# Two loads of residual rows and one set of weight casts take another place in a gated block's first feed-forward pass

## The reference, cut to what matters

```python
h = xn @ Wff1                              # 512 -> 2 x 2048
a, gate = h[..., :ff_inner], h[..., ff_inner:]
out = out + silu(gate) * a @ Wff2          # 2048 -> 512
x = x + tanh(g_xattn) * out
```

## Time and profile before

| | us |
|---|---|
| median of three executions | 2398.21 |
| the profiled execution, device time | 2401.12 |
| its span | 2399.3 |
| PE busy | 2127.6 |
| DVE busy | 1335.9 |
| ACT busy | 673.2 |
| POOL busy | 622.9 |

### The profile page before, as it was taken

How to read it: one execution, slowest core, us unless ns; L and a number is a source line. 1 busy time by engine, 2 the same in 40 slices (tenths; PEclk the granted TensorE clock), 3 DMA queues, 4 the chain that set the end, 5 groups by cost and what they waited for, 6 DMA issues and landing times. The chain is left out here.

```text
span 2399.3 us, 30019 instructions
## 1 busy us (share of the span) xinstructions
PE 2127.6 (89%) x11425; PEld 1593.7 (66%) x11425; DVE 1335.9 (56%) x2112; ACT 673.2 (28%) x1066; POOL 622.9 (26%) x552
## 2 busy tenths in 40 slices
PE   6999999999989999999999999998998435465898
PEld 5677777777668778888888888887873111121477
DVE  7665666566447777666766676666661000000377
ACT  2544554455533331112111211122430000000231
POOL 5434654464458850320032000000320000000020
PEclk9899999999999999999999999998998767687899
DMA  4223223311387659664966494434879999999767
GB/s 156 76 102 126 73 77 111 129 62 62 106 322 294 231 218 371 226 223 158 364 223 223 159 369 159 160 127 149 316 275 430 427 427 428 428 428 426 290 228 263
DMA packets 182380, 565.13 MB, mean 236 GB/s; under 512 B 15304, under 2 KB 98792, under 8 KB 152392
## 3 DMA queue, kind: packets, MB, share of 16 engines
q1 hardware_dynamic: 172936, 504.37, 55.7%
q10 hardware_dynamic: 9312, 58.99, 6.0%
HBM read 450.07 MB, written 113.25 MB: 235 GB/s over the span
## 5 line engine op out<-in xcount | busy, mean ns | idle before, releaser
L1444 PE MATMUL ff_down<-w,u 128*128 128x512 f32 x1536 | 363.7, 395 | 9.4 <-DVE ff_x L1717 9.3
L1384 PE MATMUL ff_up<-ff_t,w 128*128 128x512 f32 x1488 | 357.7, 389 | 2.3 <-ACT ff_gate L1517 2.3
L1444 PEld LDWEIGHTS ff_down<-w,u 128*128 128x128 f32 x1536 | 292.1, 191 | 74.7 <-DVE ff_x L1717 13.6
L1384 PEld LDWEIGHTS ff_up<-ff_t,w 128*128 128x128 f32 x1488 | 279.2, 188 | 60.6 <-issue 2.7
L1717 DVE SCALAR_TENSOR_TENSOR ff_x<-ff_down,gates,ff_x 128x512 f32<-128x512 f32 x256 | 191.1, 749 | 88.1 <-PE ff_down L1444 86.5
L2500 PE MATMUL e_down<-e_w,e_ug 128*32 128x512 f32 x480 | 76.7, 797 | 183.8 <-DMA e_w<-in_L_ffn_e_W 104.0
L1384 PE MATMUL ff_up<-ff_b,w 128*128 128x512 f32 x954 | 234.3, 389 | 0.0
L1384 PEld LDWEIGHTS ff_up<-ff_b,w 128*128 128x128 f32 x954 | 179.1, 188 | 37.2
L2500 PEld LDWEIGHTS e_down<-e_w,e_ug 128*32 128x32 f32 x480 | 18.7, 141 | 240.6 <-issue 131.1
L1509 ACT ACTIVATE ff_gate<-ff_gate 128x512 f32<-128x512 f32 x62 | 39.2, 633 | 410.9 <-DVE ff_gate L1693 410.9
L2604 DVE TENSOR_TENSOR e_u_rows<-e_turned,e_b1T 128x128 f32<-128x128 f32 x16 | 4.7, 292 | 266.4 <-PE e_turned L2491 266.4
(11 more groups left out here) (449 smaller groups left out, 4307.3 us busy)
## 6 DMA issues: line engine op xcount, KB each, us to landing
w<-ff_w_factors SPq DMA_DIRECT2D x48, 1792.0 KB, 7.6
e_wg<-in_L_ffn_e_Wg SPq DMA_DIRECT2D x15, 4096.0 KB, 29.1
e_w<-in_L_ffn_e_W SPq DMA_DIRECT2D x14, 4096.0 KB, 24.1
e_w<-in_L_ffn_e_W ACTq DMA_DIRECT2D x13, 4096.0 KB, 49.8
ff_w_factors<-w SPq DMA_DIRECT2D x15, 1792.0 KB, 7.2
w<-ff_w_parts SPq DMA_DIRECT2D x48, 512.0 KB, 5.3
ff_t<-ff_t_factors SPq DMA_DIRECT2D x16, 1024.0 KB, 13.9
e_w<-in_L_ffn_e_W SPq DMA_DIRECT2D x16, 1024.0 KB, 10.1
```

The costliest lines, as they stand in the source:

```text
L1384: last = nc.tensor.matmul(bank[:, :], a, m, start=start and c == 0, stop=stop and c == 5)
L1444: last = nc.tensor.matmul(DN[m % 2][:, :], a, w, start=c == 0, stop=c == 5)
```

## The change

Two things move in the first feed-forward pass. SP waits for the stores of x1 and issues both `load_x(0, i)` ahead of `keep_w1(0)`, where these came behind `keep_w1(2)`. ACT does `high_a(3)`, the casts of the fourth group's weights, behind `finish(2)`, that is behind the gates of groups 1 and 2, where they stood ahead of both; `high_s(3)`, which stood between `group(2, True)` and `finish(2)`, now follows it.

```diff
@@ sync
             for i in (S2_T2, S1_T1, S3_T3, A22_T4):
                 load_factor(i, 0)
+            x1_out, all_stores = x1_begun
+            sp.wait_ge(x1_out, all_stores)
+            for i in range(2):
+                load_x(0, i)
             keep_w1(0)
...
             load_raw(4)
             keep_w1(2)
-            x1_out, all_stores = x1_begun
-            sp.wait_ge(x1_out, all_stores)
-            for i in range(2):
-                load_x(0, i)
             keep_w2(0)
@@ scalar
             group(1, True)
+            group(2, True)
+            finish(2)
             high_a(3)
-            group(2, True)
             high_s(3)
-            finish(2)
             high_w2(2)
```

## The result

The changed kernel took 2409.01 us, median of 7 executions (2400.22 to 2412.20), against 2398.21 us (2394.54 to 2405.01) for the kernel before. The ratio is 1.0033, 95% interval 1.0022 to 1.0044. It is slower by some 8 us, where 2400.5 us was forecast.

The account below looks back on a forecast made before the run. PE, busy 89% of the span, was taken to bound the feed-forward stage. +0.3 us at group 3 and +2.0 at down(1) on 2401.12 gave 2403.4, less 2.9 for the median 2400.5 us; range 2393.5 to 2405.5.

Parts of the forecast that it names:

- The first wait, for ACT: At group 2's fourth product, PE's 2.27 us wait for ACT's silu goes, with 0.1 us of clock.
- The row loads and their price: At down(0), the 3.12 us wait for rows goes, but PE stops 6.0 us for POOL; group 3 starts 0.3 us later.
- The push on the raw weights: In the DMA queue, two early row loads make group 3's raw weights land 5.3 us later, at 704.55.
- the clock's cost: In down(0), the clock falls behind the 6.0 us stop and costs 1.7 us, bounds 0.1 and 3.4.
- What is late next: ACT's gates of group 3 come 2.6 us late, so PE waits 2.0 us in down(1), bounds 0 and 3.1.
- R3: Rival, chance 0.15: POOL falls behind, PE also waits for low parts of groups 3 and 4; 2404.6 us, 2406 with another clock fall.
- The range: For the whole kernel's time, 8 in 10: 2393.5 to 2405.5 us, allowing 2 us for differing medians.
- The sign behind 1668 us: A stage behind 1668 us changing its length by more than 1 us would make the whole sum wrong.
- R1: Rival, chance 0.27: the late gates don't reach PE, no wait in down(1); +0.3 us, 2398.5 us.
- R2: Rival, chance 0.08: group 3's raw weights aren't pushed back; 6.3 us gained, 2391.9 us.
- R4: Rival, chance 0.12: the push is partly absorbed, raw weights come 2 to 3 us later; 3.2 us gained, 2395 us.
- POOL catches up in a round: POOL, up to 9 us late at first, catches up within two groups and a down-projection; later rounds see none of it.

Follow-up runs that it names:

- e2: Kernel before with only ACT's casts of group 3 moved behind the gates, row loads at their old place; ratio 1.0023.
- e1: Changed kernel with ACT's casts put back ahead of the gates, so only the two row loads move; ratio 1.0008.
- e10: e7 with DVE's second residual addition ahead of the second product for u in all passes, and POOL's order of e5; 2392.89 us, ratio 0.9976.
- e7: e3 with row loads between load_raw(3) and keep_w1(1), and ACT's casts of groups 5 and 6 behind the gates of groups 3 and 4; ratio 0.9994.
- e8: e7 with POOL clearing the low parts of the weights of groups 3 to 6 instead of computing them; 2397.05 us, one execution.
- e5: Changed kernel with POOL making both low halves of the down-projection's weights ahead of group 3's sums; 2397.44 us, ratio 0.9993.
- e3: Changed kernel with the casts of group 3 between the gates of group 1 and those of group 2; 2403.21 us, ratio 1.0012.
- e4: Changed kernel with only the first row load early, the second back behind keep_w1(2); 2402.26 us, ratio 1.0005.
- before again: The kernel before, unedited, profiled once more; 2398.76 us, one execution.
- changed again: The changed kernel, unedited, profiled once more; 2403.63 us, one execution.

## Why the prediction was wrong

**The first wait, for ACT.** Right: 2.27 us went, and e2 shows that ACT's edit alone takes it.

**The row loads and their price.** Right in mechanism: PE's one stop in place of two, released by line 1621, was forecast at 6.0 us and measured at 7.2. Two terms were small. The push on the raw weights was 6.1 us, not 5.3; and the clock's cost was 2.24 us, not 1.7. Group 3 started 1.9 us late (727.06 - 673.57 = 53.49 against 51.62), not 0.3, near the top of the bounds given for it: 1.6 us that the sum lacks.

**What is late next.** The step that failed. The forecast said that ACT's gates of group 3 would come 2.6 us late because of a cast that waits for POOL (they were ready 2.3 us before they came) and that PE would wait 2.0 us in down(1). The place was right and so was the chain up to these gates. The size was wrong, 5.1 us for 2.0: the projection took 762.08 - 746.10 = 15.98 us for 10.88. Of these 3.1 are the wait itself, at the end of the bounds. The gates of group 4 were not late "in the same way": DVE waited only 0.40 us for them, and the rest had come down DVE's own queue, from the 2.37 us for the gates of group 3 and the 1.1 us more that POOL held its subtractions. The forecast had put this holding inside the bounds with either sign. The other 2.0 are a second fall of the clock. The sum had no term for that, though the same text had priced the first one; it appeared only in a rival, R3.

**The range.** It ended at 2405.5, and the bounds of the single terms had never been added: +2.3 at group 3 and +3.1 at down(1) on 2398.2 make 2403.6, the second fall 2405.6, and nothing was left of the 2 us that it meant to allow for the wander of medians. The measured median lies 10.8 us over that of before, the ratio says 7.9, and the profiles 7.0 and 8.2. The terms above account for 4.7 of the 8.5 us by which the forecast of the median was short; the rest no run here ties to the change.

**The sign behind 1668 us.** The forecast called its sum wrong if a stage behind the feed-forward changed its length by more than 1 us. In the profiled execution it did, 732.9 us against 730.3. But the repeats took 731.0 (changed) and 730.7 (before), and e1 to e10 lie between 727.4 and 732.1, so this can't be put down to the change, and as a sign it was too fine.

**R1, R2 and R4** did not happen: PE did wait in down(1), and the raw weights came 6.1 us later, not 0 (R2) or 2 to 3 (R4). **R3** named the wrong place: PE never waited for line 1616. Its price was nearer than the forecast's, by the fall of the clock that it allowed, and the blocking of DVE and POOL that it built on is what e7 and e8 show at work, in down(0) and down(1).

**Which half costs what.** Not asked ahead of the result, and the more useful question: both halves cost alone, 3.6 and 3.7 us in the profiles (1.9 and 5.5 by the ratios, the first not clear of noise), and together 7.0 to 8.2. The ACT edit frees a silu by queueing a later round's cast behind a residual addition.

**POOL catches up in a round.** Right, as far as PE shows it: behind group 5 the waits over 0.3 us of the changed kernel are those of before (0.42, 1.01, 0.70, 1.06, 0.42 us against 0.45, 1.03, 0.71, 1.05, 0.48).

## What to carry to other kernels

In a full queue like this one, moving a load ahead moves everything that it passes back; look for the consumer with the least cover, and untie it by the order of its own engine, as e5 did at no cost. A cast for a later round belongs ahead of anything that waits for PE, and behind anything that PE waits for; e3 against the changed kernel is 3 us at group 5 for one line. And a new stop on PE has to be priced with a fall of the clock behind it, each time, as a term that may come or not: it came behind stops of 1.81 (e10), 1.97 (e2) and 7.23 us, and not behind 2.27 (before) and 2.96 (e4).

## What the runs showed of the hardware

**The clock doesn't follow from the length of a wait.** Stretches behind a stop in e4, one of 2.96 us ahead of down(0) and one of 3.01 in down(1), with columns as in the earlier trace rows:

```profile
705.11:716.54 11.43, 11.29 (x49) 9.01 (x49) 7.65 (x10) 3.85 (x7) 6.35 (x6) 1.00 0.79 312
741.50:751.30 9.80, 9.80 (x36) 7.97 (x37) 7.56 (x9) 0.63 (x1) 7.74 (x6) 0.83 0.79 296
```

The first stayed at 2.4 GHz and the second fell. After 1.97 us in e2 it fell as well:

```profile
744.14:754.24 10.10, 10.10 (x36) 7.94 (x37) 8.09 (x9) 0.62 (x1) 7.43 (x6) 0.83 0.79 296
```

but not after 2.27 us in the kernel before:

```profile
701.33:706.89 5.56, 5.56 (x25) 4.58 (x25) 5.47 (x7) 2.32 (x4) 5.42 (x5) 1.00 1.06 406
```

The Trainium skill (TensorE: Matmul & The Clock Gate, section What's actually happening) calls the clock's watch free-running, so that a transition depends on where in it a matmul lands; these rows agree, and show nothing of the watch itself.

**The clock also falls where PE has no idle time.** Near the end of the feed-forward stage, first in the kernel before, then in e3, with columns as in the earlier trace rows:

```profile
1640.00:1665.00 25.00, 24.46 (x218) 20.41 (x217) 12.87 (x30) 3.26 (x8) 0.00 (x0) 0.73 0.23 85
```

```profile
1640.00:1665.00 25.00, 23.03 (x243) 19.95 (x242) 17.01 (x37) 4.07 (x10) 0.00 (x0) 1.00 0.23 85
```

The same instructions in both, again before and then e3:

```profile
1638.94 4.23 PE L1996 MATMUL slot_general<-sqT,d_wq 128*128 128x16 f32 x32
1643.01 5.47 PE L1444 MATMUL ff_down<-w,u 128*128 128x512 f32 x12
```

```profile
1643.43 3.64 PE L1996 MATMUL slot_general<-sqT,d_wq 128*128 128x16 f32 x32
1646.92 3.03 PE L1444 MATMUL ff_down<-w,u 128*128 128x512 f32 x12
```

In the kernel before the granted clock fell between 1641 and 1642 us, within 32 small matmuls (128x16) that stood back to back, and the two tiles behind them took 5.4 us; in e3 it did not fall, and they took 2.95.

The edits of e3 don't reach this stretch. From the start of group 5 to the last projection's wait of 1.97 us for DVE, near 1666 us, the kernel before took 913.7 us, before again 912.6, the changed kernel 912.8, changed again 907.6 and e3 907.8: 5.3 us between two executions of one kernel, which hide or feign an effect of the size studied here. One profile of a whole kernel can't tell 5 us. A distance between two marks around the change does better: it repeated within 0.1 us for the kernel before and within 1.2 for the changed one.
